# Ranking the tokens chunk by chunk inside the first attention layer

## The chip, the core and the metric

The kernel runs on one core of a Trainium2 chip. The metric is the device time of one launch in microseconds (us). A core has five engines with an instruction queue each: TensorE (PE; its weight loads are listed as PEld), VectorE (DVE), ScalarE (ACT), GpSimd (POOL) and SyncE (SP), which here only issues DMAs. Engines wait for each other through semaphores.

## What is computed

The input x has two batches (B = 2) of 2048 tokens of width 512. Four layers follow each other. The change touches the first and the second one.

```
layer 1: x1 = x + tanh(g0) * xattn(LN(x), ctx)          16 heads of 32, 128 context rows per batch
layer 2: scores = LN(x1) @ w_router                     one number per token
         _, idx = top_k(scores, 256)                    per batch; the order of idx matters (causal mask)
         x_sel  = LN(x1)[idx]; attention among the 256 tokens, gated MLP; scattered back into x1
layer 3: cross attention again, 16 heads of 64
layer 4: ternary MLP with a depthwise convolution, activations quantised to int8
```

The order of `idx` is by falling score, ties by token number. The kernel doesn't sort: a token's rank is the number of tokens with a higher score, plus the number of earlier tokens with an equal one. Where a rank is below 256, the token goes to that place.

## The kernel before, in words

**Layer 1** is `narrow_attention(LAYER0)`. A step is 512 tokens (`TILE`), so there are 8 steps, taken from the two batches in turn (`par` is the batch). A step has four slots j, one for each group of four heads. Names of this layer's tiles begin with `A_`. A slot goes like this:

- TensorE makes the scores in four PSUM banks (`SC`, L620 and L623), then a quarter of the next step's queries (`project_q`, L552). When ScalarE has taken exp of the scores (L515), it makes a rough product of the next group's scores in the same banks (`scores_for_max`, L574), the sums and the weighted values (L638, L590), and the output projection of 128 tokens of the step before (`project_out`, L561) in two halves. Between the halves it transposes the maxima (`turn_maxima`, L581).
- VectorE keeps the low part of q (L750), reduces the rough scores to maxima (`maxima`, L773 to L780; TensorE's `turn_maxima` waits for them), refines 1/sum (L790, L792), divides (L785), adds the output projection to the residual (`add_out`, L701 to L707), and finishes 128 tokens of the step before (`route`, L715 to L720: LayerNorm, router score, new residual). At j = 1 it also takes the statistics of the tile two steps ahead (`ln_stats`), at j = 2 it applies them (`ln_apply`), at j = 3 it does two `route`s.
- ScalarE also keeps the high part of q (L477), guesses 1/sum by Ln and Exp (`guess_rz`, L486, L488), and copies the turned maxima (`keep_mT`, L472; the next slot's scores need them). At j = 3 it copies the four transposed pieces of the tile two steps ahead (`keep_xT`, L464, L468; transposes L543), which TensorE's single bank `TX` makes one at a time.
- GpSimd makes rstd (L409, L419), the low part of those pieces (`low_x`, L414) and adds the output bias (L452). The next step's first `project_q` waits for the last `low_x`.
- SyncE stores each finished step: new residual (L376), normalised tokens (L378), and the router scores (L379, 4 bytes a token) to DRAM. Steps 2 to 5 run in a loop in hardware, the others are written out.

**Between layers 1 and 2** stands `choose_tokens`, whose tiles begin with `B_`. SyncE loads the scores back, once as 32 rows and once per batch copied to all partitions (`s_row`, 128 x 2048), then constants, then the context weights of layer 3, then the weights of layer 2. For each chunk of 128 tokens the whole row of 2048 scores is compared with the chunk's own scores, one per partition. VectorE does ten chunks of each batch by a compare that counts as it goes (L1733, L1736); ScalarE does six, with Relu of the difference and Sign with a sum (L1770, L1773). Equal scores inside the chunk are counted on VectorE (L1738). Then come the ranks, one-hot rows `hot` (L1749, 16 per batch), a product with token numbers on TensorE (L1710), the indices (L1752 to L1757), and 8 gathers from DRAM on GpSimd (L1795). TensorE makes layer 3's keys and values in between (`ContextStage.multiply`, L194, L198), and ScalarE keeps one tile of them after each of its chunks (L209, L227).

**Layer 2** is `choice_layer` (tiles `C_`); it begins with the norm of the gathered rows (L1839) and the qkv projection (L1897), and waits for all seven of its weight loads first. Each stage is a block; at its end all engines meet in a barrier, and its semaphores are cleared.

## Time and profile before

| what | us |
|---|---|
| median of 3 runs | 2013.34 |
| lowest, highest | 2002.27, 2016.18 |
| the profiled execution | 2013.11 |
| its span, first to last instruction | 2011.4 |
| granted TensorE clock, mean over the span | 0.913 |
| PE, DVE, ACT, POOL busy | 1607.4, 1308.4, 853.9, 553.2 |

The span is cut into 40 slices of 50.3 us in the page's second part. These are its first 16 slices, up to 805 us:

```
PE   5788898885326878
DVE  3577877785681242
ACT  3443444440561451
PEclk9899999998667898
DMA  4012222112801133
```

A digit is the busy share of a slice in tenths. Layer 1 reaches into slice 10; slices 11 and 12 are `choose_tokens`.

### The profile page before, as it was taken

Reading aid. Unit: us, or ns where it says so; the run is one execution under the profiler, and the core shown is the slowest. Engines: PE = TensorE matmul, PEld = TensorE weight load, DVE = VectorE, ACT = ScalarE, POOL = GpSimd, SP = SyncE. Lnnn points to the kernel's source line nnn. Section 1 sums busy time; section 2 is a strip of 40 time slices with the busy share of each in tenths; the row PEclk is TensorE's granted clock in tenths of the full one; section 3 lists DMA queues with packets and bytes.
Section 4 is the critical chain, followed back from the end, with each engine's and each line's share of the span. In section 5 each row is a group of like instructions: output and inputs, shape, how many; then the busy total and the mean of one; then the engine's idle time right before and its main releaser. Section 6 shows DMA issues by size and latency. Waiting matters only on the chain. (4 is left out here: it accounts for less than half of the span.)

```text
span 2011.4 us, 24639 instructions
## 1 busy us (share of the span) xinstructions
PE 1607.4 (80%) x9027; PEld 926.4 (46%) x9060; DVE 1308.4 (65%) x2080; ACT 853.9 (42%) x1325; POOL 553.2 (28%) x480
## 2 busy tenths in 40 slices
PE   5788898885326878985699999999997357888887
PEld 3444444432213563433466666566664233444443
DVE  3577877785681242413467767677766359999996
ACT  3443444440561451302533433334333047777674
POOL 3122222221011220001401201211200058777771
PEclk9899999998667898996899999999999789999999
DMA  4012222112801133514101011111010140111211
GB/s 162 19 42 85 84 83 83 63 64 84 325 12 31 63 108 106 172 47 152 42 1 62 33 53 58 39 53 53 22 53 32 33 166 22 58 58 58 72 70 43
DMA packets 77675, 144.33 MB, mean 72 GB/s; under 512 B 12529, under 2 KB 21925, under 8 KB 77050
## 3 DMA queue, kind: packets, MB, share of 16 engines
q1 hardware_dynamic: 76602, 139.68, 19.8%
q0 software_dynamic: 960, 3.15, 0.5%
q8 instruction: 71, 1.16, 0.3%
q14 instruction: 42, 0.34, 0.1%
HBM read 99.78 MB, written 43.03 MB: 71 GB/s over the span
## 5 line engine op out<-in xcount | busy, mean ns | idle before, releaser
L2405 POOL TENSOR_TENSOR E_y<-E_y,E_centre 128x1024 f32<-128x1024 f32 x64 | 151.7, 2370 | 11.8 <-ACT E_y L2432 9.7
L2330 PE MATMUL E_OP<-E_w2q,E_yb 128*128 128x512 bf16 x509 | 130.0, 414 | 26.1 <-ACT E_yb L2417 21.7
L1149 ACT ACTIVATE D_oT<-D_OB 128x512 fp32r<-128x512 f32 x64 | 38.3, 599 | 226.2 <-DVE D_OB L1495 226.2
L2321 PE MATMUL E_HP<-E_xT,E_w1q 128*128 128x512 bf16 x482 | 119.2, 387 | 11.4 <-DMA E_w1q<-w1b_d 6.5
L2397 POOL TENSOR_SCALAR E_centre<-E_hs,E_cw,E_cb 128x512 f32<-128x512 f32 x64 | 108.0, 1688 | 63.9 <-DVE E_hs L2477 63.6
L1460 DVE TENSOR_TENSOR D_q_low<-D_PJ,D_q_high 128x512 fp32r<-128x512 f32 x62 | 42.9, 692 | 115.8 <-ACT D_q_high L1125 115.5
L1227 PE MATMUL D_PJ<-D_xT_high,D_wq_high 128*128 128x512 f32 x248 | 106.1, 428 | 9.7 <-DVE D_wq_low L1467 7.2
L2486 DVE SCALAR_TENSOR_TENSOR E_y<-E_hs,E_cw,E_y 128x512 f32<-128x512 f32 x128 | 107.3, 878 | 0.0
L561 PE MATMUL A_TX<-A_wo,A_oT 128*128 128x512 f32 x192 | 102.6, 664 | 3.7 <-DVE A_res L701 3.7
L1227 PE MATMUL D_PJ<-D_xT_high,D_wq_low 128*128 128x512 f32 x248 | 99.3, 400 | 0.0
L1227 PE MATMUL D_PJ<-D_xT_low,D_wq_high 128*128 128x512 f32 x248 | 98.7, 398 | 0.0
L2330 PEld LDWEIGHTS E_OP<-E_w2q,E_yb 128*128 128x128 bf16 x512 | 52.7, 105 | 97.0 <-ACT E_yb L2417 26.6
L1235 PE MATMUL D_ZB<-D_wo_high,D_oT 128*128 128x512 f32 x256 | 90.4, 415 | 5.1 <-DVE D_rz L1509 2.9
L515 ACT ACTIVATE A_probs<-A_SC 128x512 f32<-128x512 f32 x128 | 66.0, 601 | 65.9 <-PE A_SC L623 65.9
L2424 ACT ACTIVATE E_centre<-E_hs,E_cw 128x512 f32<-128x512 f32 x64 | 46.0, 719 | 100.2 <-DVE E_hs L2477 98.3
L2339 PE MATMUL E_YT<-ident,E_y 128*128 128x128 f32 x512 | 67.1, 274 | 26.4 <-DVE E_am L2495 21.9
L1235 PE MATMUL D_PJ<-D_wo_high,D_oT 128*128 128x512 f32 x256 | 86.5, 399 | 0.3 <-DVE D_res L1403 0.3
L2477 DVE TENSOR_TENSOR E_hs<-E_HP,E_rs 128x1024 f32<-128x1024 f32 x64 | 77.6, 1212 | 5.9 <-PE E_HP L2321 5.9
L2495 DVE TENSOR_REDUCE E_am<-E_YT 128x4 f32<-128x1024 f32 x64 | 77.8, 1216 | 1.6
L2123 PE MATMUL C_PS<-C_hT,C_w 128*128 128x512 f32 (+1 forms) x176 | 77.6, 604 | 0.9 <-PEq L2057 0.9
L1266 PE MATMUL D_OB<-D_probs,D_V 128*32 128x512 f32 x512 | 70.8, 626 | 9.0 <-DVE D_oT L1501 9.0
L2339 PEld LDWEIGHTS E_YT<-ident,E_y 128*128 128x128 f32 x512 | 57.9, 141 | 42.4 <-ACT E_y L2443 18.1
(341 smaller groups left out, 3973.3 us busy)
## 6 DMA issues: line engine op xcount, KB each, us to landing
A_x<-in_x SPq DMA_DIRECT2D x8, 1024.0 KB, 5.2
A_res<-in_x SPq DMA_DIRECT2D x8, 1024.0 KB, 6.7
x_d<-A_res SPq DMA_DIRECT2D x8, 1024.0 KB, 4.3
xn_d<-A_xn SPq DMA_DIRECT2D x8, 1024.0 KB, 8.0
W_raw<-in_w1T SPq DMA_DIRECT2D x16, 512.0 KB, 4.5
W_raw<-in_w2T SPq DMA_DIRECT2D x16, 512.0 KB, 4.2
D_x<-x_d SPq DMA_DIRECT2D x8, 1024.0 KB, 5.7
D_res<-x_d SPq DMA_DIRECT2D x8, 1024.0 KB, 6.4
```

Source lines behind the costliest of these rows:

```text
L561: mm = pe.matmul(out_banks[c], oT[par][:, k, c * P:(c + 1) * P], wo[:, k, :], start=k == 0, stop=k == QT - 1)
L1227: mm = pe.matmul(bank[:, :], w[:, k, m * P:(m + 1) * P], x[:, k, :], start=k == 0 and x is xh and w is wqh, stop=k == KD - 1 and x is xl)
L1235: mm = pe.matmul(bank, o[i][:, k, c * P:(c + 1) * P], w[:, k0 + k, :], start=k == 0 and o is oh and w is woh, stop=k == OT - 1 and o is ol)
L2123: mm = pe.matmul(PS[0:w, z + m % 2, :], wt[:, k, m * P:m * P + w], hT[:, k, :], start=k == 0, stop=k == KD - 1)
L2321: mm = pe.matmul(HP[:, i % 2, e, :], w1q[:, k, m * P:(m + 1) * P], XT[n % 2][:, k, :], start=k == 0, stop=k == KD - 1)
L2330: mm = pe.matmul(OP[:, :], yb[:, k, c * P:(c + 1) * P], w2q[:, k, :], start=k == 0, stop=k == MC - 1)
L2339: mm = pe.transpose(YT[:, c, e, :], Y[i // MP % 2][:, 2 * (i % MP) + e, c * P:(c + 1) * P], ident[:, :])
L2397: pool.tensor_scalar(U[i % 2][:, 0, :], hs[i % NBUF][:, 0, 1:TILE + 1], cw[:, 2 * p, 1:2], cb[:, 2 * p:2 * p + 1], ALU.mult, ALU.add).then ...
L2405: pool.tensor_tensor(y, y, U[i % 2][:, :, :], ALU.add).then_inc(t0, 1)
L2477: dve.tensor_tensor(hs[i % NBUF][:, :, 1:TILE + 1], HP[:, i % 2, :, :], RS[n % 2][:, :].rearrange("p (a t) -> p a t", a=1).to_broadcast([P ...
L2486: dve.scalar_tensor_tensor(out=Y[n % 2][:, m, :], in0=hs[i % NBUF][:, e, 2:TILE + 2], scalar=cw[:, m, 2:3], in1=Y[n % 2][:, m, :], op0=ALU ...
L2495: dve.tensor_reduce(am[:, :, i % MP], YT[:, :, :, :].rearrange("p c e x -> p c (e x)"), AX.X, ALU.max, apply_absolute_value=True).then_inc ...
```

## The change

Everything that `choose_tokens` did up to the gathers now happens inside `narrow_attention`, which is no longer shared with a variant that nothing used. Its steps are all written out, and it takes batch 0's four steps first, then batch 1's. `choose_tokens` becomes `prepare_choice`, which only makes layer 3's keys and values and waits for the gathers.

Slots are numbered s = 4 n + j over all steps n. Chunk q (0 to 31) passes through fixed slots: in slot q + 6 TensorE turns its scores into a row (`turn_row`) and ScalarE keeps it; in slot q + 7 it is compared; chunks on ScalarE take their second pass in slot q + 8; the column sums come one or two slots later. A chunk is compared only with the chunks up to itself, (cc + 1) * 128 columns for chunk cc of its batch. The row that says which of the earlier tokens are lower counts for both sides: its own sum goes into the chunk's rank, and its column sums (products with a vector of ones, one for each earlier chunk, `sum_lower`) go into the earlier tokens' ranks (`later`). Odd chunks are ScalarE's, even ones VectorE's, except that the last two change places. After slot 31 come 12 slots that hold the rest of the ranking only, beside the last step's four `add_out` and `route`.

The router scores stay on the chip; nothing is stored or loaded for them. Layer 2's last three weights have a semaphore of their own, for which its output projection waits.

```diff
+def on_act(q):
+    return (q % 2 == 1) != (q >= NB * NC - 2)
+def before(q):
+    return max((i for i in range(q) if on_act(i) == on_act(q)), default=None)
 @ narrow_attention, schedule
+        def row_at(s):
+            return s - 6 if 0 <= s - 6 < CHUNKS else None
+        def compared_at(s):
+            return s - 7 if 0 <= s - 7 < CHUNKS else None
+        def marked_at(s):
+            return s - 8 if 0 <= s - 8 < CHUNKS and on_act(s - 8) else None
+        def summed_at(s):
+            return [q for q in (s - 9, s - 8) if 0 <= q < CHUNKS and q % NC and on_act(q) == (q == s - 9)]
+        def hot_slots(b):
+            return range(25, 29) if b == 0 else range(SLOTS + 9, SLOTS + 10)
+        def found_slot(b):
+            return hot_slots(b)[-1] + 1
+        VIRTUAL = found_slot(NB - 1) + 2
 @ GpSimd, after the last post_rstd
+            def gather(b):
+                pool.wait_ge(id_ok, 2 * (b + 1))
+                for par in range(2):
+                    pool.wait_ge(stored[par], 32 * LAPS // NB * (b + 1))
+                for h in range(b * HALVES, (b + 1) * HALVES):
+                    for out, src in ((chosen["xs"], "xn2_d"), (chosen["base"], L["out"])):
+                        pool.indirect_dma_start(...).then_inc(chosen["got"], 16)
 @ ScalarE
+            def keep_row(s):      # wait row_mm
+                    act.activation(s_row[:, b, cc * P:(cc + 1) * P], row_ps, ACT.Copy).then_inc(row_kept, 1)
+            def keep_sums(s):     # for q in summed_at(s): wait sum_mm
+                    act.activation(later[:, b, cc, 0:cc], sum_ps[:, 0:cc], ACT.Copy).then_inc(sum_kept, 1)
+            def differ(s):        # wait row_kept, lower_act
+                    act.activation(above[:, 0:w], s_row[:, b, 0:w], ACT.Relu, bias=own[:, q:q + 1], scale=-1.0)
+            def mark(s):          # wait above_ok, sum_mm of the chunk before
+                    act.activation(lower[1][:, 0:w], above[:, 0:w], ACT.Sign, accum_out=less[:, q:q + 1])
+            for s in range(SLOTS):
...
+                guess_rz(s + 1)
+                mark(s)
+                turn_x = j == GROUPS - 1 and n + 2 < STEPS
+                if turn_x:
+                    keep_xT(n + 2, 0)
+                    keep_xT(n + 2, 1)
+                if s + 1 < SLOTS:
+                    keep_mT(s + 1)
+                keep_row(s)
+                keep_sums(s)
+                keep_found(s)
+                if turn_x:
+                    keep_xT(n + 2, 2)
+                    keep_xT(n + 2, 3)
+                differ(s)
+            for s in range(SLOTS, VIRTUAL):
+                mark(s)
+                keep_row(s)
+                keep_sums(s)
+                keep_found(s)
+                differ(s)
 @ TensorE; rank_free and the first half of the slot
+            def turn_row(s):      # wait p_done q + 1, row_kept
+                    pe.transpose(row_ps, own[:, q:q + 1].to_broadcast([P, P]), ident[:, :]).then_inc(row_mm, 1)
+            def sum_lower(s):
+                for q in summed_at(s):
...
+                    need(pe, sum_kept, sums_done(q) - 1)
+                    for i in range(q % NC):
+                        mm = pe.matmul(sum_ps[:, i:i + 1], marks[:, i * P:(i + 1) * P], one[:, :], start=True, stop=True)
+                    mm.then_inc(sum_mm, 1)
+                pe.wait_ge(m_te, s + 1)
+                rank_free(s - 1)  # rows, sums and indices of the slot before are out of SC
...
+                    project_out(n - 1, j, 0, 2)
+                    if s + 1 < SLOTS:
+                        turn_maxima(s + 1)
+                turn_row(s)
+                sum_lower(s)
+                find_tokens(s)
+                if turn_x:
+                    transpose_x(n + 2, 2)
+                if n:
+                    project_out(n - 1, j, 1, 2)
+                if turn_x:
+                    transpose_x(n + 2, 3)
 @ VectorE
+            def compare(s):       # wait row_kept
+                dve.scalar_tensor_tensor(out=ties_at[:, :], in0=s_row[:, b, cc * P:w], scalar=own[:, q:q + 1],
+                                         in1=following[:, :], op0=ALU.is_equal, op1=ALU.mult,
+                                         accum_out=ties[:, q:q + 1]).then_inc(tied, 1)
+                if not on_act(q):
+                    if before(q):
+                        dve.wait_ge(sum_mm, sums_done(before(q)))
+                    dve.tensor_scalar(lower[0][:, 0:w], s_row[:, b, 0:w], own[:, q:q + 1], None, ALU.is_lt, ALU.add,
+                                      accum_out=less[:, q:q + 1]).then_inc(lower_dve, 1)
+            def choose(s):        # ranks of a batch, then its 16 hot rows over hot_slots(b), then idx
+            for s in range(SLOTS):
...
+                if n and j == GROUPS - 1:
+                    route(n - 1, SUB - 1)
+                compare(s)
+                choose(s)
+            for s in range(SLOTS, VIRTUAL):
+                c = s - SLOTS
+                if c < SUB:
+                    add_out(STEPS - 1, c)
+                    route(STEPS - 1, c)
+                compare(s)
+                choose(s)
 @ SyncE, per step
-                if post == "route":
...
-                    sp.dma_start(io["scores_d"]..., rt[par][:, :], allow_slow_non_contiguous=True)
 @ choose_tokens becomes prepare_choice
-                sp.dma_start(s_rc[:, :], io["scores_d"]...).then_inc(rows, 16)
-                ... both broadcasts of scores_d, three constants
                 stage.load(sp)
                 prefetch(sp)
...
-                compare(0)
-                compare(1)
+                stage.keep_k(act)
                 stage.high_k(act)
+                stage.keep_v(act)
...
+                pool.wait_ge(chosen["got"], 16 * 2 * NB * HALVES)
 @ choice_layer
-                dve.wait_ge(w_in, 16 * 7)
+                dve.wait_ge(w_in, 16 * 4)
```

## Rows read from the trace of the kernel before

**Rows 1.** Stretches of the span: us, busy (instructions) per engine, PEclk, DMA share, GB/s

```profile
164.00:410.00 246.00, 217.27 (x1403) 110.60 (x1401) 196.72 (x321) 102.66 (x179) 61.80 (x58) 0.94 0.22 77
506.89:612.98 106.09, 31.55 (x137) 18.52 (x137) 73.40 (x194) 59.92 (x85) 12.46 (x9) 0.63 0.46 174
```

**Rows 2.** Order of time, end of layer 1 to layer 2: start, us, instruction, [idle before]

```profile
489.66 0.75 DVE L720 SCALAR_TENSOR_TENSOR A_res<-A_xn,gates,A_res 128x512 f32<-128x512 f32 x1
506.89 0.36 SPq L1691 DMA_DIRECT2D B_s_rc<-scores_d  x1
525.83 4.47 PE L194 MATMUL B_kps<-D_ctxT,D_wk 128*128 128x256 f32 x10 [10.92 <-DMA D_wv<-in_Wv]
592.30 4.29 DVE L1749 TENSOR_SCALAR B_hot<-B_places,B_rank 128x256 bf16<-128x256 f32 x16
596.65 1.01 PE L1710 MATMUL B_ips<-B_tok,B_hot 128*128 128x2 bf16 x32 [28.15 <-DVE B_hot L1749]
598.57 1.23 POOL L1795 DMA_INDIRECT C_xs<-xn_d,C_idx  x1 [8.72 <-DVE C_idx L1757]
607.62 0.95 POOL L1795 DMA_INDIRECT C_base<-x_d,C_idx  x1 [0.30 <-issue]
612.98 0.69 DVE L1839 CUSTOM_DVE_ANT_0 C_hn<-C_xs 128x512 f32<-128x512 f32 x1 [14.70 <-PEq L57]
624.11 30.14 PE L1897 MATMUL C_PS<-C_hT,C_wqkv 128*128 128x512 f32 x64 [0.69 <-ACT C_hT L1909]
```

**Rows 3.** Groups of 499 to 613 us by form: count, busy us, mean ns, idle before

```profile
L198 PE MATMUL B_kps<-D_wv,D_ctxT 128*128 128x512 f32 x24 | 14.8, 766 | 6.2 <-ACT D_kT L209 6.2
L194 PE MATMUL B_kps<-D_ctxT,D_wk 128*128 128x256 f32 x48 | 14.7, 472 | 17.1 <-DMA D_wv<-in_Wv 10.9 <-ACT D_kT L209 6.2
L1738 DVE SCALAR_TENSOR_TENSOR B_junk<-B_s_row,B_s_col,B_before 128x128 bf16<-128x128 f32 x32 | 15.2, 476 | 0.5
L1736 DVE TENSOR_SCALAR_CACHE_REDUCE B_junk<-B_s_row,B_s_col 128x2048 bf16<-128x2048 f32 x2 | 4.7, 2345 | 0.0
L1736 DVE TENSOR_SCALAR_CACHE_REDUCE B_junk<-B_s_row,B_s_col 128x1024 bf16<-128x1024 f32 x2 | 2.6, 1276 | 0.0
L1770 ACT ACTIVATE B_ahead<-B_s_row,B_s_col 128x1920 f32<-128x1920 f32 x2 | 3.8, 1882 | 0.0
L1773 ACT ACTIVATE B_marks<-B_ahead 128x1280 bf16<-128x1280 f32 x2 | 2.5, 1270 | 0.1
L1773 ACT ACTIVATION_READ_ACCUMULATOR B_marks<-B_ahead 128x1 f32 x24 | 4.5, 186 | 0.0
L209 ACT ACTIVATE D_kT<-B_kps 128x256 f32<-128x256 f32 x8 | 2.9, 366 | 8.7 <-PE B_kps L194 8.7
```

**Rows 4.** Order of time on TensorE, slots j = 0 and j = 2 of one step

```profile
270.59 0.79 PE L552 MATMUL A_PJ<-A_xT_high,A_wq_high 128*128 128x512 f32 x1 [2.96 <-POOL A_xT_low L414]
304.60 0.52 PE L581 MATMUL A_SC<-identb,A_m 128*128 128x128 bf16 x4 [3.82 <-DVE A_m L780]
```

**Rows 5.** Order of time on VectorE, in the same step

```profile
286.61 0.75 DVE L750 SCALAR_TENSOR_TENSOR A_q_low<-A_PJ,A_bq,A_q_high 128x512 fp32r<-128x512 f32 x1 [2.91 <-ACT A_q_high L477]
300.11 0.75 DVE L750 SCALAR_TENSOR_TENSOR A_q_low<-A_PJ,A_bq,A_q_high 128x512 fp32r<-128x512 f32 x1
303.09 1.19 DVE L778 CAST A_m<-A_mx 128x16 bf16<-128x16 f32 x1
```

**Rows 6.** Order of time on ScalarE, slots j = 3 and 0

```profile
260.54 0.58 ACT L464 ACTIVATE A_xT<-A_TX 128x512 f32<-128x512 f32 x1
279.99 0.60 ACT L472 ACTIVATE A_mT<-A_SC 128x512 bf16<-128x512 bf16 x1 [1.88 <-PE A_SC L581]
```

**Rows 7.** Order of time, GpSimd beside VectorE at two places

```profile
301.74 2.48 POOL L452 TENSOR_TENSOR A_res<-A_res,A_bo 128x512 f32<-128x512 f32 x2
...
585.26 4.60 POOL L232 TENSOR_TENSOR D_k_low<-D_kT,D_k_high 128x2048 fp32r<-128x2048 f32 x1 [96.83 <-ACTq L1688]
585.56 4.45 DVE L1738 SCALAR_TENSOR_TENSOR B_junk<-B_s_row,B_s_col,B_before 128x128 bf16<-128x128 f32 x1
```

More of the change, by code:

```diff
@@ L554, in project_q, with project_out @@
                 mm.then_inc(q_mm, 1)
-            def project_out(n, par, c, part, parts):
+            def project_out(n, c, part, parts):
                 if part == 0:
@@ L594, in _, with rank_free @@
+            def rank_free(s):
+                rows = [q for q in map(row_at, range(s + 1)) if q is not None]
+                sums = [q for i in range(s + 1) for q in summed_at(i)]
+                need(pe, row_kept, len(rows))
+                need(pe, sum_kept, len(sums))
+                need(pe, id_kept, sum(found_slot(b) <= s for b in range(NB)))
             for c in range(SUB):
@@ L759, in _ @@
+            ln_stats(0)
+            ln_apply(0)
             for k in range(KD):
```

734 lines of the change are left out of this document (316 added, 418 removed).

## The prediction, made before the changed kernel was run

> **What bounds the kernel now.** I read the page's slices first. VectorE and TensorE share layer 1, but in slices 11 and 12 TensorE is at 2 to 3 tenths and its clock at 6 to 7. The table of stretches says how long that is: from SyncE's first load of `choose_tokens` to layer 2's first norm 106.1 us pass, with TensorE busy for 31.5 of them and VectorE for 73.4 [rows 1, 2]. So this stretch is bound by ranking, and layer 1 is the place to look at next, since the ranking moves there. In layer 1 VectorE works 196.7 of 246 us and ScalarE 102.7, while TensorE's records cover 217.3 [rows 1]. Such shares don't say what added work costs, so I went through one middle step in order of time, engine by engine, and asked in each slot who waits last. There are four different answers:
>
> - j = 0: TensorE never stops once `project_q` has begun; VectorE waits 2.91 us for the next queries [rows 5].
> - j = 1: VectorE gets to the next `keep_q_low` with no idle time, because `ln_stats` came in between; TensorE waits 3.82 us for the maxima in j = 2 [rows 4, 5]. VectorE decides.
> - j = 2: both are about even.
> - j = 3: ScalarE runs from `guess_rz` into `keep_xT` without a pause [rows 6], TensorE's transposes wait for it, and at the end `project_q` waits 2.96 us for GpSimd's last `low_x` [rows 4]. ScalarE decides.
>
> **What falls away between the layers.** What is left is `prepare_choice`. Before, the context weights stood behind 2.2 MB of score rows and constants, and the first product began 18.9 us after the stage's start [rows 2]. Now 3.5 MB instead of 5.7 MB lie ahead: at 355 GB/s, which 5.7 MB in some 16 us suggest, 10 us and 2 us for issue and landing, so 12. The products are 48 of 256 columns and 24 of 512 [rows 3]. A stream of 64 with 512 columns took 30.14 us, 0.471 each, its slow beginning included [rows 2]. So 24 x 0.471 + 48 x 0.236 = 22.6 us. They took 29.5 in busy time before, at a mean clock of 0.63, broken up by waits for ScalarE, which kept a tile only between its compares [rows 1, 3]. Those waits go: a tile's copy takes 0.37 against 1.4 us for its products [rows 3]. With 1.5 us for the last copy and the barrier (before, layer 2 began 4.4 us after the last gather's issue ended, most of it the landing) the stage takes 36.1 instead of 106.1: **minus 70.0**. GpSimd's `low_k`, 4.60 us [rows 7], runs under the V products. The gathers of both batches will have landed by then. The split of the weight semaphore costs nothing, the loads being done in either case; without that cover it would save a few us, never cost.
>
> **What comes on at the end of layer 1.** Call the end of the last `route` T. Before, it was 490.4, and the next stage began at 506.9, 16.5 us later, behind SyncE's wait for its stores [rows 2]. Now the last four chunks hang on it, each with its widest row. From T: VectorE's compare of chunk 28 (1664 columns, 1.95 between the rows for 1024 and 2048, plus 0.35 for ties [rows 3]) ends at 2.5; its sums reach ScalarE at 3.1; only then does ScalarE's queue let chunk 29 through both passes (1.78 and 1.70, and 0.19 to read the sum) until 7.0, keep row 31 at 7.3, and do chunk 30 (1.88, 1.80, 0.19 [rows 3]) until 11.3. VectorE does chunk 31 (2.35) in its shadow. Two sums with a copy after each: 13.3. Ranks, five small operations: 14.1. 16 one-hot rows, 4.29: 18.4. 32 products, 1.01: 19.5. Indices: 20.3. Four gathers at the pace of (607.62 - 598.57) / 7 = 1.29 us: 25.6. Barrier, as a guess between 0.8 and 3: 2. In all 27.6, **plus 11.1**. Nothing shorter covers it: the stores have long landed. Bounds: 22 if ScalarE's passes and the sums interleave better, 33 if every handover costs half a us more.
>
> **What the ranking costs inside the slots.** Small parts first. `turn_row` is one transpose, about 0.2 us. A ones product comes at 1.01 / 32 = 0.03 us [rows 2], some 8 per sum: 0.25. `keep_row` copies 128 columns: 0.25, extended from 0.37 for 256 and 0.60 for 512 [rows 3, 6]; `keep_sums` 0.2. VectorE pays 0.35 + 0.08 in every slot for ties and on average 1.28 + 0.08 for 1024 columns in odd slots [rows 3]. ScalarE pays one pass of about 1.2 in even slots (`differ`) and one of 1.2 + 0.19 and a gap, 1.45, in odd ones (`mark`).
>
> - j = 0, plus 1.5. Two sums share one place in PSUM, so TensorE's second waits until ScalarE has copied the maxima (from 279.99, 0.60 [rows 6]), the row and the first sum: second sum at 281.15, `project_out`'s second half at 281.4 instead of before 280. VectorE's 0.43 falls into its 2.91 of idle time. `differ` ends before the next scores are ready.
> - j = 1, plus 0.2 for the row on TensorE, and VectorE's 1.8 goes straight into the 3.82 us wait. But the small CAST there took 1.19 us, held until GpSimd's two bias additions (301.74, 2.48 us) were over [rows 5, 7]; coming later it will not be held. Net plus 0.9, from 0 for a narrow chunk to 1.9 for the widest. ScalarE's `mark` falls into an idle time as at j = 0, 1.88 there [rows 6].
> - j = 2, plus 1.5, as at j = 0. VectorE's 0.43 is behind TensorE's delay.
> - j = 3, plus 1.9: `mark` stands ahead of the first `keep_xT`, 1.45; `keep_row` ahead of the third, 0.25; `turn_row` 0.2. All of it moves the last `low_x`. VectorE's 1.8 hides in its wait for the queries behind it.
>
> That is 6.0 us in each of steps 2 to 5, 24.0 in all, and 0.8 in slots 6 and 7. In steps 6 and 7 neither ScalarE nor VectorE has a tile ahead to prepare: there the even slots cost 1.5 each, but 0.7 where chunk 16 has no sum; slot 25 costs 3.2 of VectorE's time (compare of 384 columns, five small operations, 4 hot rows at 0.27), 26 another 0.4, 27 with two `route`s 2.5; then 1.2 for the products of slot 29, 1.1 for the compare there, and 1.95 for the one of slot 31, ahead of an `add_out` that TensorE waits for. With the 0.2 of the odd slots: 8.5 and 7.2. Among the last four `route`s, one wide compare and three of ties lie on VectorE's path: 2.7. **Plus 43.2**.
>
> What is removed from layer 1 gives nothing I can see: SyncE's store of scores lies on no engine's path, and the hardware loop's slots are as long as those written out. More stores and loads don't arise; three constants more are loaded, behind which VectorE waits once, under a microsecond.
>
> **The sum.** The profiled execution took 2013.1 us (span 2011.4), as good as the median of 2013.3. 2013.1 - 70.0 + 11.1 + 43.2 = **1997.4 us**, 0.8% less. Faster or slower by over 1% means below 1993 or above 2033; a measurement of this kernel, with runs from 2002 to 2016, can tell hardly less.
>
> **Rivals.**
> 1. The slots hide most of it. The ends of the second sum and of `mark` are my reading of queues; if TensorE's stalls overlap with the waits it has anyway (3.82 and 2.96 us a step [rows 4]), a step costs 2.5 instead of 6.0, and steps 6 and 7 half: 43 becomes 22, the time **1976**. For it: those waits are there. Against: they end by VectorE and ScalarE, the engines that get the work.
> 2. TensorE's clock, the case on the slow side. The granted clock is 0.94 in layer 1's middle and was 0.63 in the broken-up stage between the layers [rows 1]; after the wait of 2.96 us the next product took 0.79 [rows 4]. Two new stalls of 1 us in a step and 2 more at j = 3 could keep it at the lower level (1.2 instead of 2.4 GHz) for half of each slot: some 3 us a slot over 17 to 20 slots, 50 us, **2047**. It decides from where the granted clock of steps 2 to 5 falls below about 0.8. Against it: the wait of 3.82 us is there now, and the mean is still 0.94.
> 3. GpSimd holds VectorE. A 128-column ties compare took 4.45 us while a 4.60 us GpSimd operation ran [rows 7], and 0.35 otherwise. At j = 1 the compare comes just as GpSimd begins two rstds and two bias additions, four us of work. If it comes second, each of steps 2 to 5 loses up to 3 us more at the place where VectorE decides: plus 12, **2009**. The Trainium skill (GPSIMD Engine Reference, section 1, Specifications) says the same of VectorE instructions with two SBUF inputs, the ties compare being one: by that rule the outcome depends on which of the two starts first, and the 4.45 us agree with it.
> 4. The change does not shorten the stretch as it says, because the weights and not the ranking bound it: loads contend with the prefetch, and products begin at 20 us instead of 12. **2005**.
>
> A second rule speaks against the alternation. Chunks on ScalarE need two passes: the Sign over 1280 columns takes 1.27 us and the Relu about as much, where VectorE's one compare takes 1.54 between its two rows [rows 3]. The Trainium skill (ScalarE: Activation LUTs, Rules for kernel authors) gives relu to VectorE. Followed, j = 3 would lose its 1.45 on ScalarE, 6 us over four steps, and VectorE would pay as much again at j = 2, so the sum would stay near 1997.
>
> **Chances.** Forecast 0.45, of which 0.13 ends below 1993 (its own range, 1984 to 2012: the bounds of the last chunks and 1.5 us a step); rival 1 0.25; rival 3 0.13; rival 4 0.05; rival 2 0.12. Faster by over 1% 0.38, within 1% 0.50, slower 0.12. The range leaves out rival 2 and the far end of rival 1: 1974 to 2024.
>
> **What would show it.** Layer 2's first norm should start 36 us after the first load of the context weights, that load 27 to 28 us after the last `route`, and the last `route` at about 534 us instead of 490. In a middle step the second sum should wait for ScalarE about 0.7 us, TensorE's wait at j = 2 should be near 5 us, and the first `keep_xT` should stand behind `mark`. The forecast is wrong if steps 2 to 5 grow by less than 3 or more than 9 us each, if a ties compare takes over 1 us at j = 1, or if the granted clock in layer 1 changes by more than 0.05.

## The result, and the profile after

| | before | after |
|---|---|---|
| median, us | 2011.52 (4 runs, 2002.27 to 2016.18) | 1985.72 (4 runs, 1979.90 to 1988.71) |
| profiled execution, us | 2013.1 | 1986.3 |
| its span, us | 2011.4 | 1984.5 |
| granted clock over the span | 0.913 | 0.919 |

The ratio is 0.987, with a 95% interval from 0.983 to 0.992: 1.3% faster. The forecast was 1997.4 with a range of 1974 to 2024. The time lies in the range, 11.7 us below the number (11.1 for the profiled execution), and on the far side of the bound of 1%: "within 1%", which the prediction held likeliest with 0.50, is not what came. It lies about midway between the forecast and the 1976 of rival 1, so the total by itself decides nothing between these two.

SyncE's first store of each step's outputs cuts layer 1 into seven intervals, and the first load of the context weights ends it. By these marks the two profiled executions differ so:

| stretch | before | after | change | predicted |
|---|---|---|---|---|
| first to last store (slots 8 on, and the last four `route`s) | 326.8 | 359.4 | +32.6 | +42.4 |
| last store to the context loads | 16.4 | 28.1 | +11.7 | +11.1 |
| context loads to layer 2's first norm | 106.1 | 36.5 | -69.6 | -70.0 |
| all the rest | 1562.1 | 1560.5 | -1.6 | +0.8 |

The prediction's 43.2 are these 42.4 and 0.8 for slots 6 and 7, which lie ahead of the first store. So of the 11.1 us between forecast and profiled execution 9.8 are in one place, the slots of layer 1. Interval by interval, in us:

| interval | 1 | 2 | 3 | 4 | 5 | 6 | 7 |
|---|---|---|---|---|---|---|---|
| before | 55.2 | 54.2 | 54.9 | 54.7 | 47.0 | 41.2 | 19.8 |
| after | 55.6 | 58.1 | 58.9 | 60.5 | 54.0 | 48.5 | 23.8 |
| growth | 0.4 | 4.0 | 4.1 | 5.9 | 6.9 | 7.3 | 4.1 |
| predicted | 6.0 | 6.0 | 6.0 | 6.0 | 8.5 | 7.2 | 2.7 |

These are rows of the table of stretches: length, busy time (instructions) of each engine, granted clock, DMA share and GB/s. First the kernel before, intervals 1 to 4 and 5 to 7; then the changed kernel, the same two, and the stretch that answers to the second of [rows 1].

```profile
163.67:382.52 218.85, 190.12 (x1217) 97.28 (x1216) 176.29 (x292) 91.59 (x160) 55.76 (x52) 0.94 0.21 72
382.52:490.50 107.98, 88.97 (x520) 38.94 (x518) 82.28 (x145) 31.20 (x55) 18.02 (x20) 0.94 0.23 79
```

```profile
163.58:396.70 233.12, 196.52 (x1337) 102.69 (x1337) 178.86 (x341) 114.33 (x214) 55.89 (x52) 0.92 0.18 68
396.70:522.98 126.28, 99.81 (x646) 45.62 (x644) 98.49 (x204) 47.12 (x99) 21.04 (x22) 0.89 0.18 67
551.09:587.56 36.47, 23.63 (x72) 15.54 (x72) 0.00 (x0) 7.37 (x13) 4.51 (x1) 0.77 0.96 383
```

Read first what VectorE did in intervals 1 to 4. It got 49 instructions more, 25 compares of some 16 us and the reads of their sums, and its busy time rose by only 2.6 us. Something else must have become shorter. The groups of that stretch name it: the normalisation in `route` took 11.4 us in all and takes 8.6, the product with the router's weights 12.0 and 11.1, and the CAST in `maxima` 10.8 and 3.5. These are the CAST's groups (count, busy us, mean ns, idle before), before, after, and in a kernel that leaves the ranking out (experiment 4):

```profile
L778 DVE CAST A_m<-A_mx 128x16 bf16<-128x16 f32 x16 | 10.8, 678 | 0.8
```

```profile
L912 DVE CAST A_m<-A_mx 128x16 bf16<-128x16 f32 x16 | 3.5, 218 | 0.6
```

```profile
L911 DVE CAST A_m<-A_mx 128x16 bf16<-128x16 f32 x16 | 9.4, 587 | 0.6
```

Read then the last row of the table of stretches: between the layers the DMA engines are busy for 0.96 of the stretch, at 383 GB/s.

Where TensorE waited in intervals 1 to 4 is in the view of waits (who waited, tile and line, for whom: us in total, times, longest), first before, then after.

```profile
PE A_SC L581 <- DVE A_m L780: 15.4, 4, 4.2
PE A_PJ L552 <- POOL A_xT_low L414: 5.9, 2, 3.0
PE A_PJ L552 <- issue: 5.6, 2, 2.8
PE A_TX L543 <- ACT A_xT L464: 1.7, 4, 0.4
```

```profile
PE A_SC L657 <- DVE A_m L914: 13.6, 5, 4.1
PE A_PJ L629 <- POOL A_xT_low L440: 11.4, 4, 2.9
PE A_TX L620 <- ACT A_xT L495: 6.7, 4, 2.3
PE A_SC L688 <- ACT A_later L531: 4.9, 7, 0.9
```

The growth of 14.3 us is in these rows: TensorE's busy time +6.4, the wait for `keep_xT` +5.0, the new one for the copy of the first sum +4.9, for `low_x` -0.1 (before, it is two rows), for VectorE's maxima -1.8. The last is the surprise: the wait on the engine that got the new work became shorter.

In one middle step these waits stand on TensorE (start, us, instruction, idle before and what ended it); they answer to [rows 4].

```profile
275.08 0.77 PE L629 MATMUL A_PJ<-A_xT_high,A_wq_high 128*128 128x512 f32 x1 [2.85 <-POOL A_xT_low L440]
...
285.06 0.34 PE L688 MATMUL A_SC<-A_one,A_lower 128*128 128x1 bf16 x8 [0.75 <-ACT A_later L531]
...
309.88 0.61 PE L657 MATMUL A_SC<-identb,A_m 128*128 128x128 bf16 x4 [3.53 <-DVE A_m L914]
...
324.74 0.63 PE L620 MATMUL A_TX<-ident,A_x 128*128 128x128 f32 x4 [1.90 <-ACT A_xT L495]
```

And this is VectorE at j = 1, before and after. The first fence answers to the place just ahead of [rows 5].

```profile
293.05 0.69 DVE L703 BATCH_NORM_STATS2 A_stats<-A_res 128x6 f32<-128x512 f32 x1
293.89 0.18 DVE L705 BATCH_NORM_AGGREGATE A_mv<-A_stats 128x2 f32<-128x6 f32 x1 [0.15 <-DVE A_stats L703]
...
294.21 1.44 DVE L715 TENSOR_SCALAR A_xn<-A_res,A_mv,A_rstd 128x512 f32<-128x512 f32 x1
```

```profile
298.62 0.69 DVE L815 BATCH_NORM_STATS2 A_stats<-A_res 128x6 f32<-128x512 f32 x1
299.35 0.18 DVE L817 BATCH_NORM_AGGREGATE A_mv<-A_stats 128x2 f32<-128x6 f32 x1
...
299.65 0.55 DVE L827 TENSOR_SCALAR A_xn<-A_res,A_mv,A_rstd 128x512 f32<-128x512 f32 x1
...
304.50 0.35 DVE L851 SCALAR_TENSOR_TENSOR A_ties_at<-A_scores_row,A_own_scores,A_following 128x128 bf16<-128x128 f32 x1
304.78 1.67 DVE L857 TENSOR_SCALAR_CACHE_REDUCE A_lower<-A_scores_row,A_own_scores 128x1408 bf16<-128x1408 f32 x1
...
309.36 0.20 DVE L912 CAST A_m<-A_mx 128x16 bf16<-128x16 f32 x1
```

The normalisation in `route` takes 0.55 us instead of 1.44, the small gap ahead of the aggregation is 0.04 instead of 0.15, and the CAST takes 0.20 instead of the 1.19 of [rows 5]. The compare costs 1.67 + 0.35, and most of it is paid back on the spot.

The two savings have different causes. The CAST's comes with the ranking: without the ranking it takes 9.4 us in the four intervals, with it 3.5, and still 3.5 when everything that was removed from layer 1 is put back (experiment 6). Before, it was long twice in each of steps 2 to 5, 1.2 us at j = 1 beside GpSimd's additions and 1.1 at j = 2 beside its `low_x`. With the ranking they no longer meet: in the step shown the CAST at j = 1 starts at 309.36, after the additions, and the one at j = 2 at 324.25, ahead of `low_x` at 325.34. The prediction counted on the first only.

For the normalisation GpSimd and SyncE show why. Before, and then after:

```profile
292.82 2.54 POOL L452 TENSOR_TENSOR A_res<-A_res,A_bo 128x512 f32<-128x512 f32 x2 [8.50 <-DMA A_res<-in_x]
```

```profile
289.74 2.53 POOL L483 TENSOR_TENSOR A_res<-A_res,A_bo 128x512 f32<-128x512 f32 x2
```

Before, GpSimd's bias additions wait 8.50 us for the load of the next residual, and when it comes they run beside VectorE's `route` of j = 1. SyncE issues that load once the stores of the step have landed: at 287.77, 14.8 us after the store at 272.98. The store of the router scores, 4 bytes a token, takes 12.7 us to land, where the 1 MB stores take 4.3 and 8.0. Without it the load is issued at 284.05, 6.8 us after the store at 277.25, and the additions are over before `route` comes.

The tail, in order of time from the last `route` on, answers to [rows 2] and to the prediction's chain:

```profile
523.14 1.94 DVE L857 TENSOR_SCALAR_CACHE_REDUCE A_lower<-A_scores_row,A_own_scores 128x1664 bf16<-128x1664 f32 x1
...
525.75 1.78 ACT L548 ACTIVATE A_above<-A_scores_row,A_own_scores 128x1792 bf16<-128x1792 f32 x1
527.56 1.70 ACT L559 ACTIVATE A_lower<-A_above 128x1792 bf16<-128x1792 bf16 x1
...
535.96 4.29 DVE L883 TENSOR_SCALAR A_hot<-A_places,A_rank 128x256 bf16<-128x256 f32 x16
540.31 1.01 PE L699 MATMUL A_SC<-A_tok,A_hot 128*128 128x2 bf16 x32 [5.42 <-DVE A_hot L883]
...
545.95 0.94 POOL L455 DMA_INDIRECT S_base<-x_d,S_idx  x1 [0.30 <-issue]
551.09 0.37 SPq L176 DMA_DIRECT2D D_ctxT<-in_ctxT  x1
```

### The profile page after: what moved, and what is told of

Same layout as the page of the kernel before. It is cut to its first block and busy times, and to the rows that moved or that the text cites. A ratio compares the mean times of both kernels' runs of the same rounds, so it can differ in the third digit from the quotient of the medians.

```text
span 1984.5 us, 25006 instructions
## 1 busy us (share of the span) xinstructions
PE 1621.1 (82%) x9331; PEld 939.8 (47%) x9331; DVE 1264.7 (64%) x2029; ACT 848.5 (43%) x1365; POOL 555.4 (28%) x482
## 3 DMA queue, kind: packets, MB, share of 16 engines
q1 hardware_dynamic: 72042, 137.55, 19.5%
## 5 line engine op out<-in xcount | busy, mean ns | idle before, releaser
L2430 POOL TENSOR_TENSOR E_y<-E_y,E_centre 128x1024 f32<-128x1024 f32 x64 | 151.6, 2369 | 12.0 <-ACT E_y L2457 10.2
L2346 PE MATMUL E_HP<-E_xT,E_w1q 128*128 128x512 bf16 x512 | 124.3, 387 | 9.1 <-DMA E_w1q<-w1b_d 6.0
L445 POOL TENSOR_TENSOR A_rstd<-A_var,minus_half 128x1 f32<-128x1 f32 x32 | 21.7, 680 | 215.6 <-DVE A_var L819 215.6
L2364 PEld LDWEIGHTS E_YT<-ident,E_y 128*128 128x128 f32 x512 | 57.9, 141 | 42.4 <-ACT E_y L2468 18.1
```

The lines of the kernel that those rows point to most:

```text
L2346: mm = pe.matmul(HP[:, i % 2, e, :], w1q[:, k, m * P:(m + 1) * P], XT[n % 2][:, k, :], start=k == 0, stop=k == KD - 1)
L2364: mm = pe.transpose(YT[:, c, e, :], Y[i // MP % 2][:, 2 * (i % MP) + e, c * P:(c + 1) * P], ident[:, :])
L2430: pool.tensor_tensor(y, y, U[i % 2][:, :, :], ALU.add).then_inc(t0, 1)
```

## The experiments

What is compared are the stretches between the marks, since each experiment touches one of them. A second profiled execution of the changed kernel says how well they repeat.

**1. The changed kernel again.**

> The changed kernel once more, for the spread of a stretch inside layer 1. All theories expect the same: last route at 522.9 us, context loads 28.2 us behind it, first norm of layer 2 36.5 us behind those, each within 0.3 us, if a difference of half a microsecond between two traces is to mean anything. If the last route moves by over 2 us, the other experiments need more than one look.

Measured: 359.5, 28.2 and 36.7 us for the three stretches, after 359.4, 28.1 and 36.5. They repeat to 0.2 us. That is too good to be the spread, though: the kernel of experiment 11 differs from the changed one only in a semaphore of layer 2's weights, and its stretch between the stores took 358.5, with 1.1 us less in the third interval. So a difference of 1 us in this stretch is nothing. The stretch to layer 2's first norm took 35.2 to 37.4 us in the kernels of 2 to 10, which leave its code alone, and everything behind that norm, which they leave alone too, 1390.3 to 1397.7 us (1400.1 in experiment 11). Whole times of single runs are therefore not compared, and where one is given, it is for the record.

**2. The scores are stored again.**

```
+ sp.dma_start(scores_d[...], own[:, SUB*n : SUB*(n+1)]).then_inc(stored[par], 16)
- need(sp, stored[n % 2], 32 * (n // 2))
+ need(sp, stored[n % 2], 48 * (n // 2))      (and the other three waits alike)
```

> The store of the router scores to DRAM is put back behind the other two stores of a step (nothing reads it). Theory A: leaving it out is what made the middle steps cheaper than predicted. With it the next residual's load waits some 6 us longer, GpSimd's first two bias additions fall on VectorE's route at j = 1 again (its first instruction 1.4 us instead of 0.55), and steps 2 to 5 grow by 0.9 us each, the last route coming at 526 to 527 us instead of 522.9. Theory B: the store never was on anyone's path, as I had predicted; the last route stays within 0.3 us, and the saving lies in the single semaphore operations that went from VectorE's queue. The tail behind the last route stays at 28 us by both.

Measured: 1999.4 us, first to last store 369.3, so 9.9 us more. The store takes 13.3 us to land, the residual is loaded 13.3 to 14.7 us after a step's first store instead of 6.8 to 7.1, and the normalisation of `route` at j = 1 is held again in some steps, up to 1.60 us. Intervals 1 to 4 grow by 3.9 us, as theory A says; it did not foresee the 6.0 behind them, 5.0 of which fall into the sixth.

**3. The separate semaphore instructions again.** Before, VectorE waited for its own statistics in two places (`ln_stats`, `add_out`) and then raised a semaphore of its own; the changed kernel only waits.

```
- dve.wait_ge(p_st, k)
+ wait_apart(dve, p_st, k, dve_passed)        (and in ln_stats)
```

> The separate semaphore instruction behind the waits of ln_stats and add_out on VectorE is put back, as the kernel before had it; nothing else. Theory: each costs VectorE the 0.1 us that the gap ahead of the aggregation shrank by, ten to a step, and part of it lies on the path: the stretch between the first and the last store of outputs grows by 2 to 4 us from 359.4. Rival: a semaphore instruction is lost in waits, and the stretch stays within 1 us.

Measured: 1996.6 us, first to last store 369.3, 9.9 us more. Intervals 1 to 4 grow by 3.1 us, within the 2 to 4 expected for the whole; the rest comes behind them, 5.3 in the sixth interval. There the trace shows what a late VectorE does besides. The rows are TensorE's, of this kernel and then of the changed one:

```profile
482.65 1.98 PE L639 MATMUL A_TX<-A_wo,A_oT 128*128 128x512 f32 x4
486.90 0.40 PE L658 MATMUL A_SC<-identb,A_m 128*128 128x128 bf16 x4 [2.27 <-DVE A_m L915]
...
488.47 3.28 PE L639 MATMUL A_TX<-A_wo,A_oT 128*128 128x512 f32 x4
```

```profile
477.96 2.62 PE L638 MATMUL A_TX<-A_wo,A_oT 128*128 128x512 f32 x4
481.07 0.40 PE L657 MATMUL A_SC<-identb,A_m 128*128 128x128 bf16 x4 [0.49 <-DVE A_m L914]
...
482.64 1.96 PE L638 MATMUL A_TX<-A_wo,A_oT 128*128 128x512 f32 x4
```

The same four products take 1.96 us in the changed kernel, and 3.28 here after a wait of 2.27. The granted clock of the sixth interval is 0.87 instead of 0.92. (1 - clock) times length, the work at full clock that is missing, is 7.0 us against 3.9; by this estimate up to 3.1 of the 5.3 us are the clock's. What made the clock fall there is not shown.

**4 to 6. The ranking left out, the two old parts put back, and each combined.** The first two choose the first 256 tokens of each batch instead of the best.

```
4:  row_at, compared_at, marked_at -> None; summed_at -> []     (no ranking)
5:  4, and edits 2 and 3
6:  edits 2 and 3 in the changed kernel
```

> Left out of the changed kernel: rows, compares, marks and column sums of all chunks (the first 256 tokens of each batch are chosen instead); the one-hot rows, the search for tokens and the gathers stay. Everything else of layer 1 is as changed: no store of scores, waits without a separate semaphore instruction, slots written out. Theory: those removals were worth about 10 us to 20 us in the slots by themselves, hidden in the growth of 32.5 us; so the stretch between the first and the last store of outputs, 326.8 us before and 359.4 after, is 309 to 318 here, and the ranking's own price in it 42 to 50. Rival: the removals only help when the ranking is there to collide with, the stretch is 325 to 330, and the price of the ranking is the 32.5 us that were seen.

> As the kernel with the ranking left out, but with the store of the scores and the separate semaphore instructions put back: the kernel before's slots, written out, with the one-hot rows. Theory: this is what the kernel before did, so the stretch between the stores is 325 to 332 us, some 12 to 18 more than without the two. Rival: without the ranking the two cost nothing, and it is within 2 us of the other.

> The changed kernel with both the store of the scores and the separate semaphore instructions put back, so that only the ranking is new. Each alone lengthened the stretch between the stores from 359.4 us by 9.8 us, 5 of them in the same interval (sixth). Theory: the 5 us are one event (GpSimd holds VectorE, TensorE then waits and its clock falls) that either brings on, so both together give 359.4 + 9.8 + 4.6 = 374, between 371 and 376. Rival: they add up, 379; other rival: both are one effect, 369 to 370.

| first to last store, us | without ranking | with ranking | difference |
|---|---|---|---|
| old parts in | 334.6 | 369.6 | 35.1 |
| old parts out | 322.3 | 359.4 | 37.1 |
| difference | 12.3 | 10.2 | |

For comparison, 326.8 in the kernel before. The theory for 4 expected 309 to 318 and its rival 325 to 330: neither; the removals are worth 12.3 us, at the low end of what the theory gave them. The kernel of 5 is 7.7 us longer than the one before: it also has the one-hot rows and the search of the first batch, in the fifth interval, which grows by 4.9, and its loop written out. The kernel of 6 came out at the second rival's 369 to 370: the two old parts cost 9.9 us each alone and 10.2 together. In intervals 1 to 4 they nearly add up, 3.9 and 3.1 alone and 5.7 together; behind them they don't, 6.0 and 6.8 alone and 4.5 together. The clock goes the same way: (1 - clock) times length over the seven intervals is 3.7 and 3.6 us above the changed kernel's with one part back, and 0.9 with both. By this estimate the clock is the larger part of what is missing from the sum; why it fell less with both back is open.

Where VectorE's delay meets TensorE the view of waits shows. The first fence is the kernel with both back, the second the one without the ranking but with both back, the third without both, all for intervals 1 to 4:

```profile
PE A_SC L660 <- DVE A_m L917: 19.5, 5, 5.7
```

```profile
PE A_SC L661 <- DVE A_m L916: 15.4, 4, 4.6
```

```profile
PE A_SC L658 <- DVE A_m L913: 10.7, 4, 2.7
```

With the old parts in, the ranking lengthens TensorE's wait for the maxima from 15.4 to 19.5; taking the old parts out shortens it by 5.9 with the ranking and by 4.7 without.

**7. The ties compare after the wide one.**

```
- ties compare, then is_lt compare
+ is_lt compare, then ties compare
```

> In a slot of VectorE the ties compare comes after the compare of the whole row instead of before it. At j = 1 that puts it into GpSimd's burst of two rstds and two bias additions. Theory A (rival 3 of the prediction): an instruction with two SBUF inputs is held until GpSimd pauses, so the ties compare takes 1 to 2.5 us at j = 1 instead of 0.35 and steps 2 to 5 lose as much each: last route at 527 to 532 us. Theory B: only long GpSimd operations hold it, and here it stays at 0.35; last route at 522.9 as now.

Measured: first to last store 361.4, 2.0 more, but none of it where theory A has it: intervals 1 to 4 took 232.4 us, 0.7 less than in the changed kernel, and the sixth took 2.1 more. At j = 1 of steps 2 to 5 the compare took 0.35, 0.37, 1.42 and 0.89 us. Rows of VectorE and GpSimd in order of time, at the longest:

```profile
307.43 1.42 DVE L856 SCALAR_TENSOR_TENSOR A_ties_at<-A_scores_row,A_own_scores,A_following 128x128 bf16<-128x128 f32 x1
```

```profile
307.43 2.53 POOL L483 TENSOR_TENSOR A_res<-A_res,A_bo 128x512 f32<-128x512 f32 x2
```

The compare takes 1.42 instead of 0.35 us where it starts beside GpSimd's additions. In the changed kernel it starts at 304.50 in this step and GpSimd at 304.68: it comes first, and takes 0.35. But at j = 1 of the last two steps it meets GpSimd's additions in the changed kernel too:

```profile
421.11 1.36 DVE L851 SCALAR_TENSOR_TENSOR A_ties_at<-A_scores_row,A_own_scores,A_following 128x128 bf16<-128x128 f32 x1
```

**8. Two places in PSUM for the column sums.**

```
- sum_ps = SC[:, 1, 0:NC];                 need(pe, sum_kept, sums_done(q) - 1)
+ sum_at(q) = SC[:, 1 + sums_done(q) % 2, P:P+NC];  need(pe, sum_kept, sums_done(q) - 2)
```

> The two sums of an even slot get a place each in PSUM, so TensorE's second sum no longer waits for ScalarE's copy of the first. Theory A (the prediction's term for j = 0 and 2): each of the ten even slots with two sums gives back the 0.6 to 0.75 us wait, last route 6 to 8 us earlier, at 515 to 517 us; behind it another 0.5 us. Theory B: the wait is cover for something else (ScalarE's copy of the maxima, which the next scores need), so TensorE waits the same time at the next scores instead, and the last route stays within 1 us of 522.9.

Measured: 1977.7 us, first to last store 354.9, 4.6 less, between the two theories. TensorE's waits for `later`, 4.9 us in intervals 1 to 4, are gone. Those intervals are only 1.2 us shorter, though (231.96 for 233.12), as TensorE's busy time rose from 196.52 to 200.50; the other 3.4 came behind them.

**9. ScalarE's mark behind `keep_xT` at j = 3.**

```
  guess_rz(s + 1)
- mark(s)
+ if not turn_x: mark(s)        (and mark(s) after keep_xT(n + 2, 3))
```

> ScalarE's mark pass of a slot j = 3 is moved behind the four copies of the transposed tokens (keep_xT); nothing else. In the changed kernel TensorE waits 1.90 us ahead of its transposes there, ended by ScalarE's copy. Theory: this wait is the mark's doing, so it falls below 0.6 us, and each of steps 2 to 5 becomes 1 to 1.5 us shorter; with that, the stretch from the first to the last store of the layer's outputs falls from 359.4 to about 354. Rival: another wait (GpSimd's low_x, VectorE's queries) takes its place, and the stretch stays within 1 us of 359.4.

Measured: first to last store 358.1, 1.3 less than in the changed kernel and 0.3 less than in that of experiment 11, where 5 were expected: no gain that stands clear of the spread, as the rival says. These are the waits and the stretch, intervals 1 to 4:

```profile
PE A_TX L622 <- ACT A_xT L495: 1.7, 4, 0.4
```

```profile
163.56:394.85 231.29, 199.99 (x1338) 105.00 (x1338) 181.84 (x341) 114.31 (x214) 55.87 (x52) 0.91 0.20 69
```

The wait went as the theory says, from 6.7 to 1.7 us. But the reason that the rival gives is wrong. It named other waits in its place, and they didn't come: the others are 13.4, 11.4 and 4.8, as before. The products became slower instead, 199.99 us busy where the changed kernel had 196.52, at a clock of 0.91 instead of 0.92, and the four intervals are 1.8 us shorter (0.8 against experiment 11, whose products took 195.29).

**10. All chunks on VectorE.**

```
- return (q % 2 == 1) != (q >= NB * NC - 2)
+ return False
```

> Every chunk is compared on VectorE in one pass; ScalarE does no mark and no differ pass of it, only the column-sum copies. Theory from the prediction: j = 3 gains about 1.5 us without mark, j = 0 and j = 2 pay VectorE's compare of 1.3 us on average, of which j = 2 shows it and j = 0 hides it in its wait for queries; the stretch from the first to the last store stays within 3 us of 359.4, and the tail from the last store to the context loads, with three wide compares of 1.9 us one behind the other on VectorE, stays within 2 us of 28.1. Rival A: ScalarE's two passes cost more than one of VectorE's everywhere, the stretch falls by over 5 us. Rival B: VectorE is the engine the step hangs on, the stretch grows by over 5 us.

Measured: 1979.1 us, first to last store 351.1, 8.4 less: rival A. Intervals 1 to 4:

```profile
PE A_SC L657 <- DVE A_m L914: 16.6, 7, 4.1
PE A_TX L620 <- ACT A_xT L495: 1.7, 4, 0.4
```

The waits for `keep_xT` (-5.0) and for the copy of the first sum (-4.9, there is only one sum in a slot now) are gone, the wait for the maxima is 3.0 longer, and TensorE's busy time is 2.0 shorter at a clock of 0.94 instead of 0.92. Together that is -8.9, and the four intervals are 8.4 shorter. By the rule of the Trainium skill that gives relu to VectorE (ScalarE: Activation LUTs, Rules for kernel authors) this is what should be done, and this run bears it out by the 8.4 us of the stretch, where the prediction had put nothing on it. The whole time, 6.6 us less in a single run, would not show it: four runs of the changed kernel span 8.8 us.

**11. One semaphore for all weights of layer 2.**

```
- wout, w1, w2: .then_inc(later_in, 16);  wait_ge(w_in, 16 * 4)
+ wout, w1, w2: .then_inc(w_in, 16);      wait_ge(w_in, 16 * 7)
```

> The weights of layer 2 are waited for together again (one semaphore for all seven loads) instead of four first and three later. Theory: the context stage is now 36.5 us long and the transfers run until about its end, so the split saves a little that it did not before: the time from the first context load to layer 2's first norm grows from 36.6 by 0.5 to 2 us. Rival, as predicted: the loads are done in either case, and it stays within 0.3 us.

Measured: 37.0 us from the first context load to the first norm, 0.3 to 0.5 more than in the two executions of the changed kernel, and inside the 35.2 to 37.4 of kernels with two semaphores. So a price is not shown. The row of the norm names what it waited for, here and in the changed kernel:

```profile
589.66 0.69 DVE L1863 CUSTOM_DVE_ANT_0 C_hn<-S_xs 128x512 f32<-128x512 f32 x1 [46.36 <-DMA C_w<-in_W2T]
```

```profile
587.56 0.69 DVE L1863 CUSTOM_DVE_ANT_0 C_hn<-S_xs 128x512 f32<-128x512 f32 x1 [45.63 <-PEq L57]
```

With one semaphore the last weight load ends the stage, with two the barrier behind TensorE does. The transfers end close to the barrier, and which of them ends the stage depends on the semaphore.

**12. What the runs point to.** All chunks on VectorE but chunk 30, two places for the sums, and the last two base gathers behind the barrier.

```
- return (q % 2 == 1) != (q >= NB * NC - 2)
+ return q == NB * NC - 2
- for out, src in ((chosen["xs"], ...), (chosen["base"], ...)):
+ for out, src in (...)[:2 - b]:          (and two gathers ahead of low_k in the next stage)
+ sum_at(q) as in 8
```

> Four edits to the changed kernel: all chunks on VectorE in one pass but chunk 30, which ScalarE does beside VectorE's 29 and 31; two places in PSUM for the column sums; the base gathers of the second batch moved behind the barrier into the next stage. Expected against the changed kernel's 1985.7 us: 8 less in the slots (all on VectorE gave 8.3), 3 to 5 less from the last store to the context loads for the shorter queue of compares and sums, and 2.5 for two gathers: about 1971, between 1967 and 1976. If the slots' gain came from TensorE's clock by chance and not from the lighter work, it is 1977 to 1982.

Measured: 1969.1 us median of 4 runs (1968.2 to 1975.6), ratio to the kernel before 0.978 with an interval from 0.976 to 0.981: 2.2% faster, some 17 us under the changed kernel's 1985.7 and within the 1967 to 1976 expected. First to last store 347.1 (-12.3), then 23.9 (-4.3), then 37.0 (+0.5). The clock of intervals 1 to 4 is 0.95. The tail's rows:

```profile
515.67 2.34 DVE L858 TENSOR_SCALAR_CACHE_REDUCE A_lower<-A_scores_row,A_own_scores 128x2048 bf16<-128x2048 f32 x1
515.69 1.89 ACT L549 ACTIVATE A_above<-A_scores_row,A_own_scores 128x1920 bf16<-128x1920 f32 x1
```

The one-hot rows begin 11.3 us after the last store (521.57) instead of 13.0, and two gathers at a pace of 1.25 us are out of the way. ScalarE's pair and VectorE's widest compare run beside each other, as meant.

## Why the prediction was right, and where it was not

**Between the layers: right.** -69.6 for -70.0. The first product begins 11.4 us after the first load (predicted 12), the 72 products take 23.8 us (22.6), and the stretch is 36.5 (36.1). What the prediction took for the bound, loads and then products, holds by little: experiment 11 shows the transfers of layer 2's weights ending about when the barrier does. "The loads being done in either case" is not so, since with one semaphore the norm waits for the last of them; a price of it is not shown.

**The tail: right, by two errors that cancel.** Counted from the last store, the last sum's copy ends at 12.1 (predicted 13.3), the one-hot rows at 17.3 (18.4), the gathers' issue at 23.9 (25.6). The barrier then took 4.2 where 2 was guessed. The guess should have come from the row it was made beside: there too layer 2 began 4.4 us after the last gather's issue ended.

**The slots: +32.6 for +42.4, and the step that failed is the last one of that part,** "What is removed from layer 1 gives nothing I can see: SyncE's store of scores lies on no engine's path". Experiment 6 puts the removals back and leaves only the ranking. Then the stretch grows by 42.8 us, against 42.4 predicted, and the removals are worth the 10.2 that remain.

That the ranking's own sum is met to 0.4 us is luck. By interval the ranking alone costs 20.0 in intervals 1 to 4 (24.0 predicted), 7.9 (8.5), 10.6 (7.2) and 4.3 (2.7): 4.6 too much in one part, 5.0 too little in the other. Two of the signs of being wrong that the prediction names for itself came. The first interval, which is step 2, grew by 0.4 us and not by 3 or more (by 3.3 with the ranking alone), and a ties compare at j = 1 took over 1 us, in the last two steps. The third did not: the clock from the first to the last store went from 0.94 to 0.91.

The store of the scores is on no engine's path, but it is on SyncE's: the load of the residual waits for it, GpSimd's additions for the load, and what GpSimd does late it does beside `route` at j = 1, where VectorE decides. The trace before had all of it: the store's 12.7 us to land, GpSimd's wait of 8.50 us for the load, and normalisations at j = 1 of up to 1.62 us where the median is 0.54. The Trainium skill (DMA: Bandwidth & Descriptors, Rules for kernel authors) says that an access whose last dimension isn't contiguous becomes a descriptor per element; 512 scores of 4 bytes are such a one, and the trace agrees: with the stores put back (experiment 2) the trace from the first store to the context loads has 4704 packets under 512 bytes instead of 493, 526 more for each of the eight stores. Each takes 12.7 to 13.6 us to land, where the 1 MB store ahead of it takes 4.2 to 4.4. The other removal, the semaphore instructions, the prediction did not cost at all: the gap they leave is 0.11 us each time, five times a step, 2.2 us in four steps, where experiment 3 gives 3.1; the other 6.8 come in intervals 5 to 7, and what brings them on is only in part known (the clock, by the estimate there).

**Inside the slots,** against the terms:

- Second sum behind the first one's copy: a wait of 0.7 us twice a step predicted; seven waits of 0.7 in four intervals, right. Experiment 8 confirms the cause. The term was larger, 1.5 for each even slot and 12 us in four steps; the waits are 4.9 of it, and TensorE's busy time grew by 5.9 with the ranking alone (experiment 6, 196.0 for 190.1), all added products and the clock included. Here the prediction has too much.
- `mark` ahead of `keep_xT`: 1.45 predicted, 5.0 / 4 = 1.25 measured, right. Experiment 9 confirms the cause, but not the worth: 5 us of waits were removed, and the stretch became 0.3 to 1.3 shorter, no more than the spread.
- VectorE at j = 1: plus 0.9 a step predicted, 3.6 in four. With the old parts in TensorE's wait for the maxima changed by 19.5 - 15.4 = 4.1, with them out by 13.6 - 15.4 = -1.8. So the term was right for the ranking alone, and the removals turned it round; they are 5.7 of the 9.7 us by which the prediction is off in intervals 1 to 4, and the other 4.0 lie outside this term. The wait at j = 2 is 3.53 in the middle step shown, where 5 was forecast; with both old parts back it is 4.62 there.
- The last steps: the last four `route`s grew by 4.1 instead of 2.7, at a clock of 0.80 instead of 0.88. The sixth interval's ranking costs 3.4 us more than its terms when the old parts are in; that the ties compare is held there, 1.36 us, can be 1.0 of it.

**The rivals.** 1 (the slots hide most of it, 22 us) is false in its cause: the waits that were there before did not take up the new work; with the ranking alone they grew, and the stretch grew by 42.8 and not by 22. That the whole time came within 10 us of its 1976 is the removals' doing. 2 (the clock) decides nothing as a whole, since intervals 1 to 4 have 0.92 after 0.94, not below 0.8. It is not nothing either: (1 - clock) times length, over all seven intervals, is 19.9 us before and 32.8 after. How much of the growth would have come without it the runs don't tell. 3 (GpSimd holds the ties compare) didn't happen in steps 2 to 5, in the step shown by 0.2 us only, but it did in the last two steps, 1.36 us each. Experiment 7 brings it on in steps 4 and 5 (1.42 and 0.89). The compare became 1.1 us longer and not 3, beside additions of some 1.25 us each, and intervals 1 to 4 not longer at all. The Trainium skill (GPSIMD Engine Reference, section 1, Specifications) names VectorE instructions in a 2-port mode or with two SBUF inputs as those that contend with GpSimd, and for the ties compare this run agrees. 4 (weights bound the stretch) is false at 12 us for the first product, though their transfers end close to it.

**The rule on relu.** The prediction weighed it as ScalarE's 1.45 at j = 3 against as much on VectorE at j = 2, and so at nothing. Experiment 10 gives 8.4 us in the slots. What was left out of that balance is the second sum: where two engines take turns, two sums fall into one slot and one waits for the other; where one engine does all, a slot has one sum. VectorE's compares at j = 0 and j = 2 show as 3.0 us more of TensorE's wait for the maxima, against 9.9 us of waits that went.

## What to carry to other kernels

A transfer that no engine waits for may still be waited for by the queue that issues the next one; before a removed DMA is costed at nothing, follow what is issued behind its semaphore, and who starts late beside whom because of it. An operation that takes 1.44 us in one place and 0.54 in another points to a collision, and a change of timing anywhere upstream can end it or bring it on. Work split over two engines for balance is to be costed with its handovers, not with its busy time alone.

## What the hardware showed that was not expected

- A wait taken off TensorE is not all won: with 5.0 us of waits gone in four intervals (experiment 9) its products took 3.5 us more, with 4.9 gone (experiment 8) 4.0 more; the spread of that figure is 1.3 (experiment 11). It is no rule: in experiment 10, 9.9 went and 3.0 came, and the products took 2.0 less. Four products of one form took 1.98 or 3.28 us in the same kernel (experiment 3).
- Two delays of VectorE cost 9.9 us each alone and 10.2 together, though in the four middle intervals they nearly add up. A single edit taken back is thus no measure of its share.
- A CAST of 128x16 elements took 0.20 us alone and 1.1 to 1.2 beside a GpSimd operation, twice in each of steps 2 to 5 before. With the ranking it no longer met them, which gave back 5.9 us of its compares' 16 in the middle intervals (9.4 to 3.5), or 6.7 with the old parts in (10.2 to 3.5).
- The barrier between stages takes 4.1 to 4.2 us from the end of the last gather's issue to the next load, in the changed kernel and in the last one.
